# The last image's softmax rows and g, transposed on TensorE through PSUM in an order of their own

## The reference

```python
theta = einsum('oc,bcn->bno', theta_w, xf) + theta_b      # 128 wide, as phi and g
phi   = einsum('oc,bcn->bon', phi_w, xf) + phi_b
g     = einsum('oc,bcn->bno', g_w, xf) + g_b
attn  = softmax(einsum('bno,bom->bnm', theta, phi), axis=-1)
y     = einsum('bnm,bmo->bno', attn, g)
z     = einsum('co,bno->bcn', w_w, y) + w_b               # then batch norm
return z + x
```

## Time and profile before

| what | us |
|---|---|
| median of 3 runs | 1564.57 |
| profiled execution, its own time | 1565.78 |
| its span, first to last instruction | 1564.0 |
| TensorE busy in the span | 1502.4 |
| VectorE busy | 904.8 |
| ScalarE busy | 757.6 |
| GpSimd busy | 285.2 |

### The profile page before, as it was taken

One profiled execution on the slowest core, in us unless ns is written; L12 is line 12 of the kernel. 1 busy time (PEld: TensorE's weight loads), 2 busy tenths in 40 slices (PEclk: granted clock), 3 DMA queues, 4 the chain that ended last, 5 costly groups with the idle time before them and its releaser, 6 DMA issues.

```text
span 1564.0 us, 25314 instructions
## 1 busy us (share of the span) xinstructions
PE 1502.4 (96%) x9348; PEld 823.0 (53%) x9348; DVE 904.8 (58%) x1200; ACT 757.6 (48%) x1205; POOL 285.2 (18%) x134
## 2 busy tenths in 40 slices
PE   7999999999999999999999999999999999999975
PEld 1454655446455454555546555454555546554464
DVE  1374664746547474664846557474574746647464
ACT  2554554555445454554545445554554545545541
POOL 0040310303112040210303113040220403103031
PEclk9999999999999999999999999999999999999997
DMA  8555656646466565645646466464656547456144
GB/s 230 155 198 150 236 165 187 228 144 230 141 212 213 157 219 150 226 164 186 216 141 234 149 208 232 138 231 145 213 188 188 196 143 241 160 187 233 49 152 144
DMA packets 160062, 288.43 MB, mean 184 GB/s; under 512 B 9776, under 2 KB 118320, under 8 KB 160048
## 3 DMA queue, kind: packets, MB, share of 16 engines
q1 hardware_dynamic: 160048, 288.24, 56.8%
HBM read 179.15 MB, written 109.05 MB: 184 GB/s over the span
## 4 chain that ended last, share of the span: by engine, by line
issue 76%; POOL 14%; PE 7%; DVE 2%; POOLq 0%; ACT 0%; DVEq 0%
POOL probs L951 14%; PE ps L424 2%; DVE x_lo L810 1%; PE ps L497 1%; PE ps L498 1%; PE ps L499 1%; DVE probs L801 1%; PE ps L440 1%; PE ps L451 1%; PE ps L467 0%; PE ps L469 0%; PE ps L468 0%; DVE x L828 0%; PE ps L511 0%; PE ps L482 0%
## 5 line engine op out<-in xcount | busy, mean ns | idle before, releaser
L951 POOL TENSOR_TENSOR probs<-probs,row_inv 128x1024 f32<-128x1024 f32 x128 | 284.5, 2233 | 1244.5 <-DVE row_inv L789 1244.5
L424 PE MATMUL ps<-windows,w_main 128*64 128x512 f32 x2048 | 481.5, 604 | 9.1 <-DMA windows<-in_x 8.2
L634 ACT ACTIVATE hidden<-ps,columns 128x512 f32<-128x512 f32 x512 | 317.5, 690 | 241.1 <-PE ps L451 128.7
L424 PEld LDWEIGHTS ps<-windows,w_main 128*64 128x64 f32 x2048 | 130.5, 136 | 306.1 <-issue 195.0
L810 DVE TENSOR_TENSOR x_lo<-x_lo,x_hi 128x1024 fp32r<-128x1024 f32 x128 | 204.6, 1625 | 13.6 <-ACT x_hi L664 13.4
L801 DVE STREAM_TRANSPOSE probs<-probs 128x1024 f32<-128x1024 f32 x128 | 156.3, 1231 | 75.4 <-PE ps L499 63.6
L764 DVE SCALAR_TENSOR_TENSOR x<-ps,columns,windows 128x512 f32<-128x512 f32 x128 | 96.0, 750 | 170.6 <-PE ps L451 151.2
L783 DVE TENSOR_REDUCE neg_max<-ps 128x1 f32<-128x1024 f32 x128 | 153.8, 1211 | 69.8 <-PE ps L484 67.6
L657 ACT ACTIVATE probs<-ps,neg_max 128x1024 f32<-128x1024 f32 x128 | 142.7, 1115 | 94.6 <-DVE neg_max L783 94.6
L497 PE MATMUL ps<-x_hi,arena 128*128 128x256 f32 x512 | 152.1, 297 | 16.8 <-DVE x_lo L810 11.2
L467 PE MATMUL ps<-x_hi,wp_hi 128*128 128x512 f32 x384 | 153.4, 399 | 0.0
(11 more groups left out here) (55 smaller groups left out, 1493.9 us busy)
## 6 DMA issues: line engine op xcount, KB each, us to landing
rows_out<-probs SPq DMA_DIRECT2D x128, 512.0 KB, 2.7
x_lo<-rows_out SPq DMA_DIRECT2D x128, 512.0 KB, 4.8
windows<-in_x SPq DMA_DIRECT2D x112, 562.0 KB, 7.2
out<-x SPq DMA_DIRECT2D x64, 512.0 KB, 3.6
windows<-in_x SPq DMA_DIRECT2D x64, 281.0 KB, 3.8
windows<-in_x SPq DMA_DIRECT2D x32, 280.8 KB, 7.0
rows_out<-g_t SPq DMA_DIRECT2D x16, 512.0 KB, 3.1
x_hi<-rows_out SPq DMA_DIRECT2D x16, 512.0 KB, 5.3
```

The costliest lines, as they stand in the source:

```text
L424: mm(ps[rows, hidden_bank(s, q), :], w_main[:, p, which, :], shifted(windows[:, w, :], unit // UNITS, half), start=True, stop=False, skip_ ...
L634: activation(hidden[:, s % 2, q, :], ps[:, hidden_bank(s, q), :], ACT.Relu, bias=b1s[:, column:column + 1]).then_inc(hidden_ready, 1)
L951: nc.gpsimd.tensor_tensor(rows, rows, row_inv[:, e].to_broadcast([P, PIXELS]), ALU.mult).then_inc(normalized, 1)
```

## The change

For image 15 alone, rows and g are transposed on TensorE, eight blocks of 128 x 128 a turn, into PSUM banks 4 and 5 (rows) and 6 and 7 (g). ScalarE rounds and VectorE splits straight from there into the same buffers, now without squares to rearrange. Each row's turn waits until the row before has been split. `exp_rows` from row 4 on waits for the turn of the row four before. The engines get an order of their own for this image, and SP issues its four output stores, 0 to 3, and nothing else. The bodies of the loop over images 0 to 14 stay as they are.

```diff
+        def pt_lo_turned(j):
+            return x1_lo[:, j % 2, :, :].rearrange("p k n -> p (k n)").rearrange("p (m c) -> p m c", m=QBLOCKS)
...
+        turned_row = ps[:, 4:6, :].rearrange("p b (m c) -> p (b m) c", c=P)
+        turned_g = ps[:, 6:8, :].rearrange("p b (m c) -> p (b m) c", c=P)
...
-            batch(BATCH - 1, False, False)
+            for j in range(QUARTERS):
+                store_quarter(LAST, j)
...
+            def turn_row(i):
+                if i == 0:
+                    pe.wait_ge(proj_biased, LAST * 6 + proj_step(0, G) + 1)
+                    pe.wait_ge(x1_ready, LAST * SLOTS + SLOTS)
+                else:
+                    pe.wait_ge(pt_split, LAST * QBLOCKS + i)
+                pe.wait_ge(normalized, LAST * QBLOCKS + i + 1)
+                for m in range(QBLOCKS):
+                    last = nc.tensor.transpose(turned_row[:, m, :], probs[:, i % ROWS_HELD, m * P:(m + 1) * P],
+                                               ident[:, :])
+                last.then_inc(row_turned, 1)
+            def turn_g():
+                pe.wait_ge(proj_biased, LAST * 6 + 6)
+                pe.wait_ge(tp_split, LAST * 4 + 4)
+                for m in range(QBLOCKS):
+                    last = nc.tensor.transpose(turned_g[:, m, :], g_t[:, m * P:(m + 1) * P], ident[:, :])
+                last.then_inc(g_turned, 1)
+            def attend_turned(j):
+                if j > 0:
+                    pe.wait_ge(out_added, LAST * 8 + 2 * j - 1)
+                else:
+                    pe.wait_ge(g_split, LAST + 1)
+                pe.wait_ge(pt_split, LAST * QBLOCKS + 2 * j + 2)
+                bank = ps[:, y_bank(j), 0:QUARTER]
+                for m in range(QBLOCKS):
+                    mm(bank, g_hi[:, m, :], pt_hi(j)[:, m, :], start=(m == 0), stop=False)
+                    mm(bank, g_lo[:, m, :], pt_hi(j)[:, m, :], start=False, stop=False)
+                    last = mm(bank, g_hi[:, m, :], pt_lo_turned(j)[:, m, :], start=False, stop=(m == QBLOCKS - 1))
+                last.then_inc(y_summed, 1)
...
-            batch(BATCH - 1, False)
+            project(LAST, 0, TH)
+            dx(LAST, 7)
+            project(LAST, 0, PH)
+            project(LAST, 1, PH)
+            project(LAST, 0, G)
+            scores(LAST, 0)
+            scores(LAST, 1)
+            project(LAST, 1, TH)
+            scores(LAST, 2)
+            project(LAST, 1, G)
+            turn_row(0)
+            scores(LAST, 3)
+            turn_g()
+            turn_row(1)
+            scores(LAST, 4)
+            turn_row(2)
+            scores(LAST, 5)
+            turn_row(3)
+            scores(LAST, 6)
+            attend_turned(0)
+            outputs(LAST, 0)
+            turn_row(4)
+            scores(LAST, 7)
+            attend_turned(1)
+            turn_row(5)
+            outputs(LAST, 1)
+            turn_row(6)
+            attend_turned(2)
+            turn_row(7)
+            outputs(LAST, 2)
+            attend_turned(3)
...
-                    act.wait_ge(row_sent[i - ROWS_HELD], (n + 1) * 16)
+                    if isinstance(n, int) and n == LAST:
+                        act.wait_ge(row_turned, i - ROWS_HELD + 1)
+                    else:
...
+            def round_turned_row(i):
+                act.wait_ge(row_turned, i + 1)
+                nc.scalar.copy(pt_hi(i // 2)[:, :, i % 2 * P:(i % 2 + 1) * P], turned_row).then_inc(pt_rounded, 1)
+            def round_turned_g():
+                act.wait_ge(g_turned, 1)
+                nc.scalar.copy(g_hi[:, :, :], turned_g).then_inc(g_rounded, 1)
...
-            batch(BATCH - 1, False)
+            round_x1(LAST, 7)
+            bias_projection(LAST, 0, TH)
+            bias_projection(LAST, 0, PH)
+            bias_projection(LAST, 1, PH)
+            bias_projection(LAST, 0, G)
+            exp_rows(LAST, 0)
+            exp_rows(LAST, 1)
+            bias_projection(LAST, 1, TH)
+            exp_rows(LAST, 2)
+            bias_projection(LAST, 1, G)
+            round_turned_row(0)
+            exp_rows(LAST, 3)
+            round_turned_g()
+            round_turned_row(1)
+            exp_rows(LAST, 4)
+            round_turned_row(2)
+            exp_rows(LAST, 5)
+            round_turned_row(3)
+            exp_rows(LAST, 6)
+            round_y(LAST, 0)
+            round_turned_row(4)
+            exp_rows(LAST, 7)
+            round_y(LAST, 1)
+            round_turned_row(5)
+            round_turned_row(6)
+            round_y(LAST, 2)
+            round_turned_row(7)
+            round_y(LAST, 3)
...
+            def split_turned_row(i):
+                dve.wait_ge(pt_rounded, LAST * QBLOCKS + i + 1)
+                cols = slice(i % 2 * P, (i % 2 + 1) * P)
+                nc.vector.tensor_tensor(pt_lo_turned(i // 2)[:, :, cols], turned_row,
+                                        pt_hi(i // 2)[:, :, cols].bitcast(F32), ALU.subtract).then_inc(pt_split, 1)
+            def split_turned_g():
+                dve.wait_ge(g_rounded, LAST + 1)
+                nc.vector.tensor_tensor(g_lo[:, :, :], turned_g, g_hi[:, :, :].bitcast(F32),
+                                        ALU.subtract).then_inc(g_split, 1)
...
+            sum_x1(LAST, 7)
+            split_x1(LAST, 7)
+            split_projection(LAST, 0, TH)
+            split_projection(LAST, 0, PH)
+            split_projection(LAST, 1, PH)
+            find_max(LAST, 0)
+            find_max(LAST, 1)
+            invert_sum(LAST, 0)
+            invert_sum(LAST, 1)
+            split_projection(LAST, 1, TH)
+            find_max(LAST, 2)
+            invert_sum(LAST, 2)
+            split_turned_row(0)
+            find_max(LAST, 3)
+            invert_sum(LAST, 3)
+            split_turned_g()
+            split_turned_row(1)
+            find_max(LAST, 4)
+            invert_sum(LAST, 4)
+            split_turned_row(2)
+            find_max(LAST, 5)
+            invert_sum(LAST, 5)
+            split_turned_row(3)
+            find_max(LAST, 6)
+            invert_sum(LAST, 6)
+            split_y(LAST, 0)
+            add_outs(LAST, 0)
+            split_turned_row(4)
+            find_max(LAST, 7)
+            invert_sum(LAST, 7)
+            split_y(LAST, 1)
+            split_turned_row(5)
+            add_outs(LAST, 1)
+            split_turned_row(6)
+            split_y(LAST, 2)
+            split_turned_row(7)
+            add_outs(LAST, 2)
+            split_y(LAST, 3)
+            add_outs(LAST, 3)
         @block.gpsimd
         def _(pool):
```

More of the change, by code:

```diff
@@ L243, in conv_attention @@
         row_landed = [sem(f"row_landed_{i}") for i in range(QBLOCKS)]
+        row_turned = sem("row_turned")
+        g_turned = sem("g_turned")
         pt_rounded = sem("pt_rounded")
@@ L258, in conv_attention @@
         TH, PH, G = 0, 1, 2
+        LAST = BATCH - 1
         PROJECTIONS = [(0, TH, 2), (0, PH, 6), (1, PH, 7), (0, G, 4), (1, TH, 7), (1, G, 6)]
@@ L485, in scores, with attend @@
                 last.then_inc(scored, 1)
-            def attend(n, j, has_next):
+            def turn_row(i):
[27 more added lines that the diff above has]
+                last.then_inc(y_summed, 1)
+            def attend(n, j):
                 if j > 0:
@@ L491, in attend @@
                     pe.wait_ge(g_split, n + 1)
-                    if has_next:
-                        pe.wait_ge(hidden_ready, (n + 1) * SLOT_PAIRS + GROUP_PAIRS)
+                    pe.wait_ge(hidden_ready, (n + 1) * SLOT_PAIRS + GROUP_PAIRS)
                 pe.wait_ge(pt_split, n * QBLOCKS + 2 * j + 2)
@@ L553, in batch @@
                 scores(n, 7)
-                attend(n, 0, has_next)
+                attend(n, 0)
                 if has_next:
@@ L561, in batch @@
                     mains(n + 1, 2, range(0, 4))
-                attend(n, 1, has_next)
+                attend(n, 1)
                 if has_next:
@@ L571, in batch @@
                     hidden_left(n + 1, 3)
-                attend(n, 2, has_next)
+                attend(n, 2)
                 if has_next:
@@ L581, in batch @@
                 output(n, 2, 1)
-                attend(n, 3, has_next)
+                attend(n, 3)
                 if has_next:
@@ L622, in _ @@
                 batch(n, True)
-            batch(BATCH - 1, False)
+            project(LAST, 0, TH)
[29 more added lines that the diff above has]
+            attend_turned(3)
+            outputs(LAST, 3)
         @block.scalar
@@ L654, in exp_rows @@
                 if i >= ROWS_HELD:
-                    act.wait_ge(row_sent[i - ROWS_HELD], (n + 1) * 16)
+                    if isinstance(n, int) and n == LAST:
+                        act.wait_ge(row_turned, i - ROWS_HELD + 1)
+                    else:
+                        act.wait_ge(row_sent[i - ROWS_HELD], (n + 1) * 16)
                 e = slice(i % ROWS_HELD, i % ROWS_HELD + 1)
```

## The result

The change took 1551.03 us (median of 4 runs, 1550.54 to 1552.55) against 1564.56 (1564.31 to 1564.86) for the kernel before, beside it on the same chip: a ratio of 0.9915 (0.9901 to 0.993), 13.5 us faster. The profiled execution took 1550.54, its span is 1548.73.

The account below looks back on a forecast made before the run. TensorE bounds the whole kernel, but waits leave holes in the last image. The walk from 1501.30 to 1547.33, plus 3.3 clock and 3.44 end, gave span 1554.1, 9.9 less: 1554.7 us, range 1551.5 to 1558.5 (0.68).

Parts of the forecast that it names:

- 1 row 0, g, row 1: After the last projection: row 0 turned, rounded, split; maximum 3, exponential 3; g rounded, split; row 1 split: 9.25 us.
- 2 rows 2 and 3: Two rows, each maximum, exponential, rounding and split in turn at 4.58 us: 9.16 us, turns and scores hidden.
- 3 exponential 6 to output(0): Maximum 6, exponential 6, copy of y and output(0) with twelve matmuls: 4.23 us, attend(0) hidden.
- 4 turn 4 to attend(1): On TensorE, row 4's turn 1.03, scores(7) 1.36 and attend(1) 2.87: 5.26 us.
- 5 turn 5 to attend(2): Row 5's turn, rounding and split, then row 6's turn and attend(2): 7.58 us, outputs(1) hidden.
- 6 turn 7 to first additions: Row 7's turn 1.25, rounding 1.10, split 1.16, first additions of quarter 2 0.95: 4.46 us.
- 7 attend(3) to the last addition: Attend(3) 3.07, copy of y 0.47, first output half 0.93, four additions 1.62: 6.09 us, ending at 1547.33.
- rival (b): Last image: split from PSUM slowed to 2.0 beside GpSimd, 1560.8 us, or transposes costing twice, 1559.9; beyond 1558.5, 0.13.
- rival (c): Last image: the clock doesn't drop at all and the walk holds as it stands, 1551.4 us; chance 0.10.
- the clock's term: Last image on TensorE: one attend (2.3) and one turn (1.0) slow at half clock, 3.3 us added to the walk.
- Rival (a): TensorE stays at half clock from the first turn to attend(3) and becomes the bound, 1569.5 us; chance 0.06.
- Rival (d): Last image no faster, because a wait left over from the loop still sets the pace, 1564.6 us; chance 0.03.

Follow-up runs that it names:

- kernel filled with scores: The change with score block 4 computed three times over into the same banks; 1550.45 us, one run.
- path alone: Turns on TensorE and PSUM banks as in the change, but every engine keeps the loop's order; 1568.12 us, ratio 1.0015 to the kernel before.
- order alone: Kernel before, with block transposes, stores and fetches kept and image 15 written out in an order of its own; 1555.63 us, ratio 0.993.
- better order: The change with another order for the last image, same steps and PSUM banks; 1544.67 us, ratio 0.9872 to the kernel before.
- kernel with the late store: The change with the last image's quarter 2 stored after quarter 3; 1552.44 us, ratio 0.9917 to the kernel before.

## Why the prediction was right

The predicted 1554.7 was 3.7 us above the measured 1551.03. That is inside the range by 0.03 only, and below the 1551.5 to 1558.5 to which the forecast gave 0.68; that it fell inside is luck. The chain that the prediction walked is another matter. Its seven steps against the trace after, from the start of row 0's turn at 1499.20:

| step | predicted | measured | ends after at |
|---|---|---|---|
| 1 row 0, g, row 1 | 9.25 | 8.93 | 1508.13 |
| 2 rows 2 and 3 | 9.16 | 9.05 | 1517.18 |
| 3 exponential 6 to output(0) | 4.23 | 4.63 | 1521.81 |
| 4 turn 4 to attend(1) | 5.26 | 5.11 | 1526.92 |
| 5 turn 5 to attend(2) | 7.58 | 7.21 | 1534.13 |
| 6 turn 7 to first additions | 4.46 | 4.19 | 1538.32 |
| 7 attend(3) to the last addition | 6.09 | 6.27 | 1544.59 |
| sum | 46.03 | 45.39 | |

Each step is within 0.4 us, and doubled turns lengthened the steps in which the walk had them, so the chain was the right one. Most of its prices hold:
- A turn was 1.03 from first to last, as taken from four transposes in 0.66, but in part by luck: what it costs TensorE ahead of the next matmul is 0.79, where the walk had 1.03, and ScalarE starts on the result 1.07 to 1.12 after the turn's start, where it had 1.25. In the run that turns g three times, 24 in a row take 2.78 us, which puts one transpose 0.109 behind another ((2.78 - 0.27) / 23), near the lower bound of 0.11. The 275 ns of the Trainium skill, "TensorE: Matmul & The Clock Gate", "Part 4: PE-mode transpose", agrees with one transpose by itself (0.27), not with a row of them; the 2.2 us for a turn did not come, and rival (b)'s doubled transposes did not either.
- The split from PSUM was 1.22 beside GpSimd's 1.89 (1.24 taken): the slowed split of rival (b) did not happen. The choice to read it from additions with one operand in PSUM, rather than from splits with both in SBUF, was the one that mattered.
- Rounding was 1.00 to 1.02 from PSUM (1.05 taken).

**The term that was mis-sized is the clock.** "One slow attend (2.3) and one slow turn (1.0): 3.3" measured 0.3, what filling the hole gave back. One spell of 0.50 came, among the first rows, where the walk had its longer holes. One turn there took 1.97 instead of 1.03, and no attend ran slow: attend(0) only ended later, which is 0.32 of the 0.40 by which step 3 is longer (it takes 4.31 in the kernel filled with scores). The path goes through ScalarE and VectorE there, and the slow matmuls ran in TensorE's idle time. From 1520 on, where attends are on the path, the clock is 1.00. The error was to price slow work as if all of it lay on the chain. So rival (c), the walk without the clock's loss, is what happened in effect, though the clock did fall; that its 1551.4 is so near to 1551.03 comes of three misses that cancel: -0.6 in the steps, +0.7 at the end, and -0.4 by which the medians moved further than the profiled tails.

The end was 4.15 (3.44 taken). The prediction took 4.97 less 1.53; the second store measured 1.31, and the other 0.5 is within what two profiled ends with the same pair of stores differ by, 4.97 and 5.46. The whole miss of 3.7 is then -3.9 to the last addition (-3.3 is the clock's term, -0.6 the steps, whose measured lengths hold the 0.3 that the clock did cost), +0.7 behind it, and -0.4 for the medians.

One sign of being wrong that the prediction named, image 15's first half moving, looks as if it had come: the last projection is 2.09 earlier. But 2.05 of it stand already at the preamble's transposes, so that half itself did not move.

Rival (a), half clock throughout, is out: the clock is 1.00 from 1520 to 1540. The Trainium skill, "TensorE: Matmul & The Clock Gate", "Part 4: PE-mode transpose", which spoke for (a), says that full clock does not engage for transposes. The trace disagrees as far as it goes: with all turns doubled TensorE runs nothing but transposes from 1502.9 to 1506.1, and the clock is 1.00 there and until 1550; whether it would rise for transposes alone no run shows. Rival (d), a wait left over from the loop, did not come in the change, but the path alone comes near it: with the loop's order kept, in the one way that was tried, nothing is gained.

What the prediction didn't see is which half of the change earns the time. It removed stores and fetches first and let the order follow. The runs say: order alone 8.65 (1.58 of it the store at the end), path alone -1.45, both 13.18. The three orders differ in detail, so these are not exact shares; that a new order earns most of the time without the new path is shown. Nor did it ask whether the strict hand-over of 4.58 a row, which it walked correctly, was needed; the better order took 7.24 more.

## What to carry to other kernels

The last iteration of a pipelined loop has no successor to fill its waits, so an order that is right inside the loop leaves holes there: write it out by hand, and look there before replacing a slow path by a fast one. On engines that run in order, a result that is ready early is worth nothing if the step that takes it stands behind another's wait. Put a clock's loss into a sum only for work on the chain, and look first whether another engine pair sets the pace in that stretch.

## What the hardware showed that was not expected

- Transposes of float32 follow one another at 0.109 us (2.78 us for 24), with 0.27 for one by itself; the matmul behind a turn of eight starts 0.79 after the turn. In the kernel with doubled turns the granted clock stayed at 1.00 over 3.2 us of nothing but transposes.
- A 1024-column VectorE step with one operand in PSUM ran at 1.22 beside a GpSimd step that kept its 1.89, where splits with both operands in SBUF took 2.0 and GpSimd 2.79.
- A slow spell of the clock can be almost free: two windows of 4 us at 0.50 and 0.71 cost 0.26 us, and a spell a little earlier in the kernel with the late store cost nothing that shows.
- The spell's place is not fixed: behind waits of 3.17 and 3.18 ahead of the same turn it slowed row 3's turn in one kernel and row 2's in the other, and a wait of 2.04 led to a fall in one kernel and to none in another.
